# Post-norm transformer pair on one core: ScalarE's wait moved to the first exponential, layer 0's normalisations on VectorE, longer listed lengths for loads

## The reference, cut to what matters

```python
x = _layernorm(x + _L0_attn_ref(x, Wq, Wk, Wv, Wo))   # 32 heads of 16, 8 key heads, RoPE, causal softmax
x = _layernorm(x + _L0_ffn_ref(x, ...))               # 4-bit packed weights, 512 -> 1376 -> 512, SiLU gate, result in fp16
x = _layernorm(x + _L1_attn_ref(x, ...))              # 512 -> 128, a two-way state-space block applied twice, 128 -> 512
x = _layernorm(x + _L1_ffn_ref(x, ...))               # int4 weights, 512 -> 1792 -> 512, SiLU gate

def _layernorm(x, axis=-1, eps=1e-05):
    m = jnp.mean(x, axis=axis, keepdims=True)
    v = jnp.var(x, axis=axis, keepdims=True)
    return (x - m) / jnp.sqrt(v + eps)
```

## Time and profile before

| what | value |
|---|---|
| median of 3 runs | 1624.26 us (1624.23 to 1624.38) |
| the profiled execution's own time | 1626.21 us |
| its span, first to last instruction | 1624.0 us |
| mean granted TensorE clock | 0.957 |
| busy PE / PEld / DVE / ACT / POOL | 1454.7 / 1081.9 / 1081.7 / 802.8 / 773.4 us |
| moved by DMA | 100.34 MB, mean 62 GB/s |

### The profile page before, as it was taken

One profiled execution on the slowest core, in us unless ns is written; L12 is line 12 of the kernel. 1 busy time (PEld: TensorE's weight loads), 2 busy tenths in 40 slices (PEclk: granted clock), 3 DMA queues, 4 the chain that ended last, 5 costly groups with the idle time before them and its releaser, 6 DMA issues.

```text
span 1624.0 us, 33859 instructions
## 1 busy us (share of the span) xinstructions
PE 1454.7 (90%) x12464; PEld 1081.9 (67%) x12464; DVE 1081.7 (67%) x2353; ACT 802.8 (49%) x1723; POOL 773.4 (48%) x918
## 2 busy tenths in 40 slices
PE   4767899978899889999999989569999999999998
PEld 2555676766676678686886857337666776857865
DVE  4898776755666667675877876757779679772121
ACT  2566666755656667675766843223333433412211
POOL 3776666566566666666222136424343343332211
PEclk9878799999999999999999999869999999999999
DMA  5433233233433232332002000450100000100000
GB/s 188 128 104 95 67 80 91 67 75 94 105 79 81 68 92 62 104 88 88 9 2 72 28 30 14 175 187 2 34 7 14 27 14 1 40 7 8 14 14 14
DMA packets 94221, 100.34 MB, mean 62 GB/s; under 512 B 11565, under 2 KB 76672, under 8 KB 94056
## 3 DMA queue, kind: packets, MB, share of 16 engines
q1 hardware_dynamic: 92818, 98.10, 21.2%
q10 hardware_dynamic: 1238, 0.07, 0.1%
HBM read 78.70 MB, written 19.43 MB: 60 GB/s over the span
## 4 chain that ended last, share of the span: by engine, by line
PE 40%; DVE 22%; POOL 13%; DMA 11%; issue 6%; SPq 5%; ACT 3%; DVEq 0%; ACTq 0%; POOLq 0%
PE ps L1703 10%; PE ps L1538 5%; PE ps L1601 4%; DMA vs<-in_s1g 4%; DMA vs<-in_s1u 3%; PE ps L1723 3%; PE ps L1553 3%; PE ps L1525 2%; PE ps L1591 2%; DVE xraw L1324 2%; DMA vs<-in_s1d 2%; POOL xr L874 2%; POOL vl L859 2%; PE ps L1651 2%; POOL vq L851 2%
## 5 line engine op out<-in xcount | busy, mean ns | idle before, releaser
L1159 DVE TENSOR_REDUCE nmax<-ps 128x1 f32<-128x384 f32 (+3 forms) x352 | 218.9, 634 | 83.1 <-PE ps L1594 79.9
L1035 ACT ACTIVATE Pe<-ps,nmax 128x256 f32<-128x256 f32 (+3 forms) x512 | 247.0, 535 | 31.3 <-DVE nmax L1159 30.2
L1029 ACT ACTIVATE pth<-ps 128x512 f16<-128x512 f32 (+1 forms) x352 | 196.7, 561 | 130.7 <-PE ps L1601 127.2
L1154 DVE TENSOR_TENSOR ptl<-ps,pth 128x512 f16<-128x512 f32 (+1 forms) x352 | 217.4, 632 | 32.9 <-ACT pth L1029 30.8
L1601 PE MATMUL ps<-identf,Pe 128*128 128x128 f32 x1280 | 208.8, 283 | 10.2 <-DVE ptl L1154 10.0
L1591 PE MATMUL ps<-kT,qT 128*128 128x256 f16 (+3 forms) x512 | 142.2, 311 | 35.1 <-ACT Pe L1035 34.5
L1601 PEld LDWEIGHTS ps<-identf,Pe 128*128 128x128 f32 x1280 | 144.6, 147 | 42.0 <-issue 20.8
L941 POOL TENSOR_TENSOR int1l<-prod,int1h 128x256 f16<-128x256 f32 x112 | 86.4, 776 | 175.6 <-ACT int1h L1115 175.6
L1703 PE MATMUL ps<-x3h,w1gh 128*128 128x256 f16 x448 | 123.3, 275 | 4.9 <-DVE prod L1394 3.8
L1703 PE MATMUL ps<-x3h,w1uh 128*128 128x256 f16 x448 | 123.4, 275 | 0.0
L1703 PE MATMUL ps<-x3l,w1gh 128*128 128x256 f16 x448 | 123.4, 275 | 0.0
(11 more groups left out here) (236 smaller groups left out, 4067.1 us busy)
## 6 DMA issues: line engine op xcount, KB each, us to landing
xr<-in_x SPq DMA_DIRECT2D x16, 256.0 KB, 4.8
x_dram<-xr SPq DMA_DIRECT2D x16, 256.0 KB, 2.0
x2a<-x_dram SPq DMA_DIRECT2D x4, 1024.0 KB, 4.8
x<-x_dram SPq DMA_DIRECT2D x4, 1024.0 KB, 5.1
out<-x SPq DMA_DIRECT2D x16, 256.0 KB, 2.0
vq<-in_q1g SPq DMA_DIRECT2D x28, 128.0 KB, 2.2
vz<-in_z1g SPq DMA_DIRECT2D x28, 128.0 KB, 3.9
vs<-in_s1g SPq DMA_DIRECT2D x28, 128.0 KB, 4.5
```

Of the source, the lines that this page charges most:

```text
L1029: act.activation(pth[:, u % 3, 0:g * w], ps[:, 2 + u % 2, 0:g * w], ACT.Copy).then_inc(sem("pth"), 1)
L1035: ins = act.activation(Pe[:, u % 2, x * w:(x + 1) * w], ps[:, u % 2, x * w:(x + 1) * w], ACT.Exp, bias=nmax[:, u % 4, x:x + 1])
L1154: dve.tensor_tensor(ptl[:, u % 3, 0:g * w], ps[:, 2 + u % 2, 0:g * w], pth[:, u % 3, 0:g * w], ALU.subtract).then_inc(sem("ptl"), 1)
L1159: dve.tensor_reduce(nmax[:, u % 4, 0:g], ps[:, u % 2, 0:g * w].rearrange("p (g w) -> p g w", g=g), AX, ALU.max, negate=True).then_inc(sem( ...
```

## The change

ScalarE no longer waits for the zeros' stores before its stream; the wait stands before the first `exp`. The last step of both normalisations of layer 0 becomes a VectorE step that comes after a GpSimd step with the power alone; the waits of `bn1` and `bn2` for the tile two before fall away, as both are now on VectorE. In the list, loads and stores, `deq` and the issue times of SP get longer lengths, a few GpSimd steps shorter ones, and VectorE and SP start later.

```diff
-            A("SP", "w0", c, 3000, [("deq", c - 2)] if c >= 2 else [], r - 6)
-            A("DVE", "deq", c, 1500 if n == HW else 1200, [("w0", c)], r)
+            A("SP", "w0", c, 6500, [("deq", c - 2)] if c >= 2 else [], r - 6)
+            A("DVE", "deq", c, 2600 if n == HW else 1900, [("w0", c)], r)
...
-            A("SP", "w1c", c, 3000, [("w1_lo", c - 2) if c >= 2 else ("w0_lo", NC0 - 1)], r - 6)
+            A("SP", "w1c", c, 5700, [("w1_lo", c - 2) if c >= 2 else ("w0_lo", NC0 - 1)], r - 6)
...
-            A("SP", "w1s", c, 2500, [("w1_lo", c)], r)
+            A("SP", "w1s", c, 3600, [("w1_lo", c)], r)
...
-            A("POOL", "attn", q, 500, [("out", q), ("atr", t - 2) if q % NOG == 0 and t >= 2 else None], u)
+            A("POOL", "attn", q, 430, [("out", q), ("atr", t - 2) if q % NOG == 0 and t >= 2 else None], u)
...
-        A("POOL", "x1", t, 1500, [("bn1", t)], r - 4)
+        A("POOL", "rstd1", t, 600, [("bn1", t)], r - 4)
+        A("DVE", "x1", t, 570, [("rstd1", t)], r - 4)
...
-            A("POOL", "x2_sum", t, 1400, [("y16", t), ("x1", t)], soon - 4)
+            A("POOL", "x2_sum", t, 1200, [("y16", t), ("x1", t)], soon - 4)
...
-            A("POOL", "x2", t, 1500, [("bn2", t)], soon - 4)
+            A("POOL", "rstd2", t, 600, [("bn2", t)], soon - 4)
+            A("DVE", "x2", t, 570, [("rstd2", t)], soon)
...
-            at[e] = t + (SP_ISSUE if e == "SP" else ns + GAP)
+            at[e] = t + (SP_ISSUE.get(name[0], 450) if e == "SP" else ns + GAP)
...
-SLACK, GAP, SP_ISSUE = 150, 0, 1300
-START_AT = {"PE": 5100, "ACT": 6400, "DVE": 12600, "POOL": 5100, "SP": 15000}
+SLACK, GAP = 150, 0
+SP_ISSUE = {"w0": 1900, "w1c": 1300, "w1s": 850, "weights_a": 4500, "weights_b": 1700, "w1_load": 1300}
+START_AT = {"PE": 5100, "ACT": 6400, "DVE": 13100, "POOL": 5100, "SP": 17500}
...
-            if kind in ("x1", "x2"):
-                n, v, r, m = ("1", ve, rstd, mv) if kind == "x1" else ("2", veb, rstdb, mvb)
+            if kind in ("rstd1", "rstd2"):
+                v, r = (ve, rstd) if kind == "rstd1" else (veb, rstdb)
                 o = key % 2
-                x = xr[:, key % RING, :]
-                pool.wait_ge(sem(f"ve{n}"), key + 1)
-                pool.tensor_tensor(r[:, o:o + 1], v[:, o:o + 1], neghalf[:, 0:1], ALU.pow).then_inc(sem(f"rstd{n}"), 1)
-                pool.wait_ge(sem(f"rstd{n}"), key + 1)
-                pool.tensor_scalar(x, x, m[:, o, 0:1], r[:, o:o + 1], ALU.subtract, ALU.mult).then_inc(sem(kind), 1)
+                pool.wait_ge(sem("ve1" if kind == "rstd1" else "ve2"), key + 1)
+                pool.tensor_tensor(r[:, o:o + 1], v[:, o:o + 1], neghalf[:, 0:1], ALU.pow).then_inc(sem(kind), 1)
...
             if kind == "exp":
+                if u == 0:
+                    for k in "gud":
+                        act.wait_ge(sem(f"st_zs_{k}"), 16)
                 act.wait_ge(sem("nmax"), u + 1)
...
             act.wait_ge(sem("consts"), 1)
-            for k in "gud":
-                act.wait_ge(sem(f"st_zs_{k}"), 16)
             act_stream(act)
...
             if kind == "bn1":
                 dve.wait_ge(sem("x1_sum"), t + 1)
-                if t >= 2:
-                    dve.wait_ge(sem("x1"), t - 1)
                 layer_norm_1(dve, own, x, st6, mv[:, o, :], ve[:, o:o + 1], sem("ve1"))
+            if kind in ("x1", "x2"):
+                m, r = (mv, rstd) if kind == "x1" else (mvb, rstdb)
+                dve.wait_ge(sem("rstd1" if kind == "x1" else "rstd2"), t + 1)
+                dve.tensor_scalar(x, x, m[:, o, 0:1], r[:, o:o + 1], ALU.subtract, ALU.mult).then_inc(sem(kind), 1)
...
             if kind == "bn2":
                 dve.wait_ge(sem("x2_sum"), t + 1)
-                if t >= 2:
-                    dve.wait_ge(sem("x2"), t - 1)
                 layer_norm_1(dve, own, x, st6b, mvb[:, o, :], veb[:, o:o + 1], sem("ve2"))
```

More of the change, by code:

```diff
@@ L908, in pool_stream @@
                 kind, key = name[0], name[1]
-                if kind in ("x1", "x2", "x2_sum", "attn", "f0_lo", "qk", "q_lo", "k_lo"):
+                if kind in ("rstd1", "rstd2", "x2_sum", "attn", "f0_lo", "qk", "q_lo", "k_lo"):
                     pool_job(pool, kind, key)
@@ L1414, in dve_stream @@
                     dve_gate(dve, kind, key)
-                if kind in ("qk_c", "qk_s", "v", "etq1", "etk1", "x1_sum", "bn1", "fxl", "bn2"):
+                if kind in ("qk_c", "qk_s", "v", "etq1", "etk1", "x1_sum", "bn1", "x1", "fxl", "bn2", "x2"):
                     dve_job(dve, own, kind, key)
```

## The result

The changed kernel took 1569.32 us (median of 4 runs, 1568.97 to 1570.86) against 1624.24 us for the kernel before. The ratio is 0.9666, with a 95% interval of 0.9649 to 0.9683: 55 us or 3.3% faster, where the prediction had 12 us and a range down to 1597. The direction was right, the size was not.

The account below looks back on a forecast made before the run. It took VectorE as the bound from 52 to 185.6 us and TensorE from there to 940. Start -6.0, normalisations +1.6, holes -6 and transition -2 made -12.4 us: 1612 us, range 1597 to 1627.

Parts of the forecast that it names:

- part 3, the lists: After 186 us: better-fitting list lengths shorten waits; -6 us together with GpSimd's relief, bounds -20 and +20.
- Part 3, the first stage: Before 186 us: the list's rank leaves the mix as it is; last unpacking about 173, first `gu` 179 us.
- Part 1, the start: First microseconds: projection begins at 8.6 instead of 16.62 us; -6 us taken, bounds 0 and -8.0.
- swallowed head start: Rival, first 186 us: weight-chunk loads leave only 1.7 us of the earlier start; 1620 us in all; chance 20%.
- Part 2, the normalisation: Layer 0's 32 steps: 66.6 us less on GpSimd, 17.5 us more on VectorE; +1.6 us before 185.6 us.
- Part 4: Transition (1037.6 to 1110 us): `yp` and `h_rs` come sooner; -2 us, within 0 and -4, up to +8 if reordered.
- VectorE's head-of-line wait: Rival, 186 to 940 us: VectorE stops at `x1`/`x2` for GpSimd's power; +33 us, 1643 in all; chance 15%.
- The new order fits much better: Rival: half of TensorE's 41 us of holes goes and the start gives its full 8; 1596 us; chance 15%.

Follow-up runs that it names:

- w1load_only: Kernel before with only the listed length of layer 1's chunk load raised, to 5700: 1576.6 us, ratio 0.972.
- w0_lists_only: Kernel before with all new list lengths except those of layer 1's chunks: 1653.9 us, ratio 1.0185.
- lists_only: Kernel before with all the new list lengths and nothing else: 1576.1 us, ratio 0.9723.
- act_only: Kernel before with only ScalarE's wait for the zeros' stores moved: 1616.9 us, ratio 0.9974.
- light_loads: Kernel before, old lists, without layer 1's loads of zeros and scales from the third chunk on (its weights wrong): 1577.9 us, ratio 0.9737.
- norm_only: Kernel before with only the normalisations' last step moved to VectorE, with its list lengths: 1606.3 us, ratio 0.9912.

## Why the prediction was wrong

**The step that failed is part 3, the lists**, taken at -6 us with bounds of -20 and +20; alone they gave -45, and the length of layer 1's load alone gave -46. Three things went wrong in it. First, it priced the waits by what TensorE's own rows name as releaser (19.2 us for exponentials, 7.9 us for `attn`). GpSimd's 44.7 us at `in_s1g` stood in the same group of rows, and part 4 of the page, with 13% GpSimd and 11% DMA on the chain, was not read. Second, the gap was read from the wrong load: 1.9 us of issue and 6.1 us to land are those of layer 0's chunks. Layer 1's load, the one that mattered, was not measured against its 3.0 us in the list. Third, the most that it allowed for was half of TensorE's 41 us of holes. `w1load_only` took away 33.3 of the 48.2 us of holes up to the last `pv`, and TensorE's busy time fell by 12.5 us besides, at a clock of 1.00 for 0.99; the prediction had taken idle time as all that a better order could give back.

That the changed kernel does more attention in the first stage is no part of the gain: `w1load_only` reached the first `gu` at 180.7 us and gained the same 46 us.

**Part 3, the first stage.** "I expect the rank to leave the mix as it is" was wrong. With the new lengths of layer 0's part the last chunk came at 196.5, not 173, and the first `gu` at 203.7, not 179 (201.8 and 209.8 in `w0_lists_only`); the trade was attention for unpacking, and it cost nothing in the end (`lists_only` and `w1load_only` have the same ratio).

**Part 1, the start: right in the main.** The projection began at 8.34 us (8.6 forecast) and `qk_c` at 15.44 (17.1): the eight wide matmuls took 5.23 us where I kept 6.68. The hole in VectorE came (7.23 us before the second `qk_c`), but otherwise than worked out: the first unpacking waited until 28.90, behind the second tile's `qk_c` and a copy that the new list puts ahead. The worth of 6 us lies between the 4 us in the kernel before and the 9 to 13 in the changed one. The swallowed head start did not come: it had 1.7 us at the first stage, where the first `gu` came at 176.8 us in `act_only` against 185.6 before (181.5 in `light_loads`, whose lists are the same up to there), and at 203.7 against 207.8 with and without the head start in the changed kernel.

**Part 2, the normalisation: the terms right, the effect partly missed.** The step takes 0.54 us at the median and 0.66 to 0.67 us in the mean, with 2.0 us at the longest, against 0.55 + 0.2 charged; GpSimd's busy time is 703.0 us against 707 forecast. VectorE's 1087.5 against 1100 hides two terms: in `norm_only` it rose by 20.7 us, to 1102.4, and in `lists_only` it fell by 8.3, to 1073.4. The comparison of 0.47 with 0.98 us at L1166 mixed shapes: 0.47 is the one piece of 96x512, while a 128x688 took 0.57 us at best and 1.20 in the mean. The longest steps agree with the rule of the Trainium skill (SBUF — State Buffer, Who interferes with whom) that the one engine waits out the other's whole instruction: those of 1.71 us (at 127.22), 1.06 us (600.94) and 2.01 us (987.85) each ended 0.29 us behind the end of the GpSimd instruction beside them (126.77 + 1.87, 600.99 + 0.72, 986.75 + 2.82). No run here took GpSimd away. Alone the move gave 14 us, where the forecast had a loss of 1.6 us and a share of the -6.

**Part 4: right in its size.** The stretch from the last `pv` to the last 514 us shrank by 3.1 us (2 forecast), and by 2.8 us in `norm_only`; VectorE's wait of 1.9 us for `yp` is gone in both. It is gone in `lists_only` too, where the stretch shrank by 1.0 us, so not all of it is shown to be the normalisation's. The last 514 us did not change.

**The rivals.** VectorE's head-of-line wait did not come: 0.7 us in one wait after, 12.1 us in nine waits in `norm_only`, which was faster all the same. "The new order fits much better" was the right case, with a price of 20 us where it measured 45 and a chance of 15%.

## What to carry to other kernels

Where the order is written by a simulated plan, compare the plan's lengths with the trace first, and above all each load from its first issue to its last landing: an engine that reaches a load too early holds up everything listed behind it. Here a length that was too long cost nothing, where one that was too short cost 3%. Read the chain that ended last for an engine or transfer that should not be on it, before reading which engine is busiest: 94% busy did not mean that TensorE set the pace. A fit that is improved in one place can make the kernel slower as long as another is wrong.

## What the runs showed of the hardware that was not expected

The same eight matmuls of 128x512 with which the projection of the first tile begins took 6.68 us in the kernel before, where they followed 10.40 idle us of TensorE, and 5.23 us in the changed one, where they followed 2.12 idle us. Those of the second tile took 3.67 us before (from 27.40 us on) and 5.37 us after (from 17.68 us on). For the second tile the recorded clock goes with the times: 1.00 before, and after 0.64 up to 20 us and 0.71 from there to 23. For the first tile the record says 1.00 in both kernels, and yet both times are longer than 3.67 us. The DMA engines were busy all through the 6.68 us (share 1.00 to 1.05), and in the 5.23 us only in its first half (0.60, then 0.02); whether that or a clock that the record misses made the difference was not tried.

The 0.29 us by which three VectorE steps ended behind a GpSimd instruction, told under part 2, are of the same kind: read from one trace, and not tried.
